# A deep-CTR tower on one core: row ids spread over the partitions by TensorE, start-up loads reordered by need, and fewer gathers between the first embeddings and the main loop

## The reference, cut to what matters

```python
e = jnp.stack([tbl_0[ids[:, 0]], ..., tbl_31[ids[:, 31]]], axis=1)   # 512 x 32 x 32
...
x0 = prev = e
for W in (filter_0, filter_1):                    # (1024, 128) and (4096, 128)
    z = jnp.einsum('bhd,bmd->bhmd', x0, prev)
    z = z.reshape(b, h * m, d)
    prev = jax.nn.relu(jnp.einsum('bpd,pn->bnd', z, W[0]))
    outs.append(prev)
z = jnp.sum(jnp.concatenate(outs, axis=1), axis=-1)        # 512 x 256
h = jnp.concatenate([z, dense_ctx], axis=1)
h = jnp.maximum(h @ W_top1 + b_top1, 0.0)
h = jnp.maximum(h @ W_top2 + b_top2, 0.0)
y = h @ W_top3
```

## Time and profile before

| | us |
|---|---|
| median of 3 runs (lowest, highest) | 889.67 (888.46, 891.25) |
| the profiled execution | 889.24 |
| its span, first to last instruction | 887.1 |
| PE busy in the span | 841.0 (95%) |
| DVE, ACT, POOL busy | 779.7, 764.0, 650.2 |
| PE's share of the chain that ended last | 89% |

### The profile page before, as it was taken

How to read it: one execution, slowest core, us unless ns; L and a number is a source line. 1 busy time by engine, 2 the same in 40 slices (tenths; PEclk the granted TensorE clock), 3 DMA queues, 4 the chain that set the end, 5 groups by cost and what they waited for, 6 DMA issues and landing times.

```text
span 887.1 us, 14536 instructions
## 1 busy us (share of the span) xinstructions
PE 841.0 (95%) x3637; PEld 678.5 (76%) x3637; DVE 779.7 (88%) x2420; ACT 764.0 (86%) x2582; POOL 650.2 (73%) x615
## 2 busy tenths in 40 slices
PE   0578999999999999999999999999999999999998
PEld 0346888888887888888888888888888888888873
DVE  2475999999999999999999999998899999999884
ACT  1239999999999999999999999999999999999872
POOL 6456888787788888888887888876766666676582
PEclk9979999999999999999999999999999999999999
DMA  7437767667767767667767666677767666675430
GB/s 181 106 75 199 176 155 163 147 153 170 161 153 168 163 152 163 147 157 166 162 153 174 161 154 161 144 164 160 160 154 170 155 155 156 143 165 106 92 72 0
DMA packets 53236, 131.20 MB, mean 148 GB/s; under 512 B 8395, under 2 KB 17875, under 8 KB 53028
## 3 DMA queue, kind: packets, MB, share of 16 engines
q0 software_dynamic: 21872, 68.43, 43.0%
q1 hardware_dynamic: 29502, 59.08, 20.3%
q10 hardware_dynamic: 1779, 2.77, 1.1%
HBM read 60.63 MB, written 3.05 MB: 72 GB/s over the span
## 4 chain that ended last, share of the span: by engine, by line
PE 89%; SPq 3%; DVE 3%; ACT 2%; DMA 2%; issue 1%; DVEq 0%
PE ya L870 14%; PE ya L872 14%; PE ya L871 14%; PE yd L870 11%; PE yd L872 11%; PE yd L871 11%; PE acc L870 3%; PE acc L872 3%; PE acc L871 3%; SPq L315 3%; ACT scaled L541 2%; DMA xb<-xt_scratch 1%; DVE emb L658 1%; DMA idx<-in_ids 1%; PE acc L899 1%
## 5 line engine op out<-in xcount | busy, mean ns | idle before, releaser
L541 ACT ACTIVATE scaled<-ya,emb 128x128 f32<-128x128 f32 x2288 | 654.3, 382 | 53.8 <-PE ya L872 46.0
L763 DVE SCALAR_TENSOR_TENSOR acc<-yd,emb,acc 128x128 f32<-128x128 f32 x1400 | 394.4, 341 | 5.9 <-PE yd L872 5.8
L406 POOL TENSOR_TENSOR quarter<-scaled 128x512 f32<-128x512 f32 x127 | 195.2, 1537 | 64.4 <-DMA scaled<-scaled 46.9
L870 PE MATMUL ya<-w_hi,prev_hi 128*128 128x512 f32 x572 | 224.8, 393 | 4.5 <-ACT scaled L541 2.5
L872 PE MATMUL ya<-w_hi,prev_lo 128*128 128x512 f32 x572 | 222.8, 390 | 0.0
L871 PE MATMUL ya<-w_lo,prev_hi 128*128 128x512 f32 x572 | 222.8, 390 | 0.0
L399 POOL DMA_DIRECT2D scaled<-scaled x127 | 116.4, 917 | 96.4 <-ACT scaled L541 91.7
L870 PE MATMUL yd<-w_hi,prev_hi 128*128 128x512 f32 x446 | 174.3, 391 | 1.0 <-DVE pooled_b L788 1.0
L872 PE MATMUL yd<-w_hi,prev_lo 128*128 128x512 f32 x446 | 173.6, 389 | 0.0
L871 PE MATMUL yd<-w_lo,prev_hi 128*128 128x512 f32 x446 | 173.5, 389 | 0.0
L381 POOL DMA_INDIRECT emb<-in_tbl,idx x112 | 123.2, 1100 | 42.7 <-issue 22.2
(11 more groups left out here) (136 smaller groups left out, 778.0 us busy)
## 6 DMA issues: line engine op xcount, KB each, us to landing
scaled<-scaled POOLq DMA_DIRECT2D x127, 512.0 KB, 8.3
xb<-xt_scratch SPq DMA_DIRECT2D x62, 512.0 KB
x<-xt_scratch SPq DMA_DIRECT2D x62, 192.0 KB
xm<-xt_scratch SPq DMA_DIRECT2D x30, 256.0 KB
scaled<-in_w ACTq DMA_DIRECT2D x4, 512.0 KB
emb<-in_tbl,idx POOLq DMA_INDIRECT x112, 3.9
xt_scratch<-xt_stage SPq DMA_DIRECT2D x7, 256.0 KB
wt_sb<-in_W_top SPq DMA_DIRECT2D x2, 512.0 KB
```

Source lines behind the costliest of these rows:

```text
L406: pool.tensor_tensor(four, piece[:, 0:C], piece[:, C:2 * C], ALU.add).then_inc(quartered, 1)
L541: op = act.activation(scaled[:, tile % PR, C * j + N * i:C * j + N * (i + 1)], a_bank(n)[:, N * i:N * (i + 1)], ACT.Copy, scale=scale_of(t ...
L763: dve.scalar_tensor_tensor(after, y_part, scale_of(tile, HB * j + i), before, ALU.mult, ALU.add).then_inc(chained, 1)
L870: pe.matmul(dst, v_hi, m_hi, start=start, stop=False)
```

## The change

Seven edits go together. `ids_across` is gone. In its place 8 KB of ids go to one partition (`ids_row`), VectorE turns them to float32 (`cast`), and TensorE multiplies them with a row of ones, which puts the ids of each half of a group on all partitions of a PSUM bank; `find` reads them there in four halves. The loads of w1 on ACT's queue wait until the small tables have landed. The ids of the later groups move from SP's queue, where they stood behind the tables, to ACT's, ahead of w1; and `number_within(1)` moves behind the first group's picks. The context's turn on TensorE moves behind the first group's candidates. `wt1_ctx` and the two biases with W_top3 (one array of 8 numbers per partition, made on the host) stay ahead of the loop; the two large tower weights move behind the loads of chunk 2 on SP's queue, and are waited for at the end. `fold_scale` rides on `pick`. GpSimd's gathers for group 1 wait for `l0_done` and are 5 where they were 13; the other 83 are spread over 80 tiles (1.04 a tile, before 0.94).

```diff
-    EARLY_NEXT = 13
+    EARLY_NEXT = 5
...
+        ids_row = sb("ids_row", [1, PICK_TILES, len(SMALL) * P], I32)
+        ones = sb("ones", [1, P])
+        ids_f32 = [xt_stage[0:1].rearrange("p g b -> p (g b)"), emb_sorted[0:1].rearrange("p g b -> p (g b)")]
+        across = [yd[:, 0, :], yd[:, 1, :], yd[:, 2, :], acc0[:]]
-        not_below = xt_stage[:].rearrange("p g b -> p (g b)")
+        not_below = sum0[:, 0, :]
...
         def _(sp):
             sp.dma_start(idx[:, 0, :], ids[0:P, :]).then_inc(ids_loaded, 16)
+            sp.dma_start(ids_row[:], ids_first...).then_inc(pick_loaded, 16)
             sp.dma_start(pick_sb[:], pick).then_inc(pick_loaded, 16)
-            sp.dma_start(ids_across[0:PICK_P], dram(ids_first, 0, [[0, PICK_P], [1, PICK_TILES * len(SMALL) * P]])).then_inc(
-                pick_loaded, 16)
...
-            sp.dma_start(idx[:, 1:BT, :], ids[P:B, :]...).then_inc(later_ids_loaded, 16)
-            sp.dma_start(wt1_sb[:], ...).then_inc(tower_loaded, 16)
...
+            sp.dma_start(wt1_ctx[:], W_top1[2 * N:2 * N + D_CTX, :]).then_inc(ctx_loaded, 16)
+            sp.dma_start(tower_small[:], biases_w3).then_inc(ctx_loaded, 16)
...
             load_l0(2)
+            sp.dma_start(wt1_sb[:], W_top1[0:2 * P, :].rearrange("(t p) n -> p t n", p=P)).then_inc(tower_loaded, 16)
+            sp.dma_start(wt2_sb[:], W_top2.rearrange("(t p) n -> p t n", p=P)).then_inc(tower_loaded, 16)
...
             pool.wait_ge(picked, PICK_TILES * len(PAIRS))
-            pool.wait_ge(gathered[0], 16 * GATHERED_LAST)
+            pool.wait_ge(l0_done, 1)
...
+            act.dma_start(idx[:, 1:BT, :], ids[P:B, :].rearrange("(t p) f -> p t f", p=P)).then_inc(later_ids_loaded, 16)
+            act.wait_ge(small_tables_loaded, 16 * len(SMALL))
             for s in range(4):
                 act.dma_start(w1_raw[:, fields, :], w1[:, fields, :]).then_inc(w1_loaded, 16)
...
-            act.wait_ge(tower_loaded, 16 * 6)
+            act.wait_ge(ctx_loaded, 32)
...
+            for bt in range(PICK_TILES):
+                pe.wait_ge(ids_cast, bt + 2)
+                for r in range(2):
+                    pe.matmul(across[2 * bt + r], ones[:], ids_f32[bt][:, C * r:C * (r + 1)], start=True, stop=True)
+                    ...
+            pe.wait_ge(small_tables_loaded, 16 * len(SMALL))
+            candidates(0)
+            ...   # the context's turn
+            candidates(1)
```

## The result

The changed kernel takes 887.76 us (median of 16 executions, 884.61 to 890.17), the kernel before 889.66 (888.18 to 891.25). The ratio is 0.9979, with a 95% interval of 0.9971 to 0.9988: 0.2% faster, which lies within the 0.3% that a measurement of this kernel can tell. Forecast were 875.5 us, with 872 to 881 as the range. The prediction was wrong by 12.3 us, and outside its range.

What follows compares the result with a forecast made beforehand. The first turn waited for picks, these for loads; TensorE bounds the loop behind. Moving the turn from 51.07 to 36.7 gains 14.4 us: span 872.7, plus 2.1 around it, 0.4 to the median, 0.3 for lateness: 875.5 us, range 872 to 881.

Steps and rivals of the forecast that it cites:

- Part 1: Ahead of the first turn: small tables, issued at 2.1 us, land 14.5 us later, at 16.5, likely 14 to 19.
- T: The time when the small tables land: forecast 16.5 us, likely 14 to 19; just under 33.17 before.
- Part 2: Work behind the small tables' landing: VectorE's picks end at 35.3 us, ScalarE's context share at 34.9.
- ScalarE: context's turn behind the candidates, T + 0.3 + 6.6 + 1.0: Context's turn, after landing to start 0.3 us and candidate matmuls 6.6; then copy and w0's rounding, 0.6 each.
- the picks' T + 18.8: VectorE's picks end 18.8 us after the small tables land, at 35.3: 17.8, 0.3 to start, 0.65 for a mask.
- Part 3: The first 24 gathers become last, landed at 36.1; first turn at 36.7 instead of 51.07, gain 14.4 us.
- The rule that the picks cost the gathers nothing: VectorE's reductions never hold the port shared with GpSimd, so gathers beside picks lose 0 us; bound at most 8.2.
- Part 4: First turn to loop stays 12.84 us, bounds -1 and +1; ScalarE's stage ahead of the full loop unchanged.
- The tower weights "0 to +1": 1 MB between loads of chunks 2 and 3, 4 to 5 us of DMA, chunk 3 wanted 20 us later: 0 to +1.
- Part 5: Gathers of later groups, spread over the loop's tiles, land in time for ScalarE's sort: cost 0, bound +1 us.
- The rivals: Tables still end it (0.20); picks or casts hold gathers (0.09); w1 ends it (0.06); picks never held the turn (0.01).
- what would show it wrong: Signs: turn waiting for `emb L670` or w1's rounding, gathers over 1.3 us before 34, or ScalarE idle before tile 20's sort.

Runs made afterwards that it cites:

- control: The changed kernel as it is, timed again on chip C beside the kernel before: 878.03 us, ratio 0.9878.
- again: The changed kernel as it is, timed once more on chip A: 878.09 us, beside 889.01 for the kernel before.

## Why the prediction was wrong, point by point

- *Part 1, T = 16.5.* Measured 16.07 in the result's trace, 14.4 to 16.1 in all traces with this order of loads. Right.
- *Part 2, what hangs on T.* This is where it failed, at "ScalarE: context's turn behind the candidates, T + 0.3 + 6.6 + 1.0" and at the picks' T + 18.8, both of which let a reader start when TensorE's matmul ends: the step put nothing for the wait between the two. Where completions come on time the terms hold: in `control` (T = 15.56) the copy starts at T + 5.7, w1's rounding at T + 8.3, and the picks end at T + 18.5. On the result's chip the copy starts at T + 19.4, w1's rounding at T + 20.4 though w1 had landed, and the picks end at T + 29.6. The last candidates are seen from 37.62 on; the second group's mask and four picks of 1.9 us each lead to 45.71 and the turn to 45.81. This costs 9.1 us against 36.7.
- *Part 3, the gathers end it, turn at 36.7.* Right where nothing is held: 35.43 and 35.84 in the two traces of the changed kernel, about 1 us early. The rule that the picks cost the gathers nothing held on every chip: 0.94 to 0.95 us each beside picks, the 24th at 32.77, earlier than the earlier trace rows. The one of 1.34 us (25.20 in `control`) lay beside L688 (25.04), which reads SBUF twice.
- *Part 4, turn to loop 12.84.* Measured 12.70. *The tower weights "0 to +1".* Mis-sized: I had asked when chunk 3 was wanted, and not how soon the x rows of chunk 2, just ahead of them on the queue, and of chunk 3, behind them, were. It cost up to 3.4 us, 1.8 and 2.5 in the two traces without the delay (45.9 and 46.6 against 44.0). The Trainium skill (DMA: Bandwidth & Descriptors, "Why a DMA increments its semaphore by 16 and not by 1"), which I had drawn on for 125 partitions, gives by the same rule three engines for these rows, whose slowest dimension is 3. No row here counts the engines: 12.5 and 17.5 us for a load of 192 KB don't speak against it, and don't show it.
- *Part 5, cost 0, bound +1.* The gathers came in time for the sort, as forecast. What I had not costed is GpSimd's own time. Before, 75 gathers over 80 tiles left tiles 0, 16, 32, 48 and 64 without one; 83 leave none free and put two into tiles 26, 53 and 79. Between banks 138 and 160 (tiles 31 to 35) this costs 2.0 us in the result's trace and 0.9 in `control`; VectorE's longer wait for GpSimd's sum (2.03 and 1.14 us, before 0.65) and its longer `small<-x` are the parts that the traces show.
- *The rivals.* None of the four is what happened. The first turn waited for `emb L670`, which the prediction had named as what would show it wrong, but not because T or the picks were slow.

Summed up: against 872.7 the span is 9.1 longer up to the turn, 0.2 shorter up to bank 0, 3.4 and 2.0 longer in the loop, 0.1 elsewhere: 887.1, measured 887.2. Where nothing is held the kernel takes 878.0, inside the range. There (`control`, span 875.5) the turn and the way to bank 0 are 1.8 us quicker than forecast, the two losses take 2.5 and 0.9, and 1.1 more goes between banks 160 and 566, which I did not trace. That the errors have different signs is luck, and so in part is the place inside the range.

What stays open: what holds the completions. Shown is that it went with the chip (887 us on chip B, 878 on A and C; chip D shows none either in the kernels run there), that it holds TensorE's completions and neither GpSimd's pace nor ScalarE's completions, and that at both places it ends when a long row of gathers ends. Chip B had a single comparison, so a chip and a state of that machine are not told apart. The profile's ends of matmuls are modelled, so it is not shown either whether the update is late or the matmul's own end; only the starts of the matmuls behind it are on time. That the gathers are the cause was only argued. The two experiments that would tell, gathers away and w1's loads away, were tried on chips where there was nothing to see, and not on chip B.

Against the gathers alone speaks that they run just as long on the other chips. The trace of the kernel before says more. By its record of semaphore events (below) it is of the same kind as the five with the delay, and its 13 gathers, from 51.73 to 71.71, run beside the first turns, layer 0 and the loop's first banks. Of the completions of TensorE that an idle engine waited for in that stretch only one is late, by 0.8 us. Its candidates start at 33.17, when its first row of gathers is nearly through (33.75), so there was little that could be held. This fits its 889 us on every chip. What the change did, then, was to move the candidates into a stretch where their completions can be late; the forecast took them over as rows of a stretch without that.

## What to carry to other kernels

A time that hangs on another engine's completion should be given a margin where the change moves it beside a long row of indirect DMAs (a precaution: the cause is not shown), and a change should be timed on more than one chip: here a gain of 11 us on two chips was 2.7 us on another. When a load is moved, ask for each later transfer on its queue how large its window is, the smallest first; a single buffer refilled once a chunk was the first to go late here. On an engine that has little time to spare, ask what tiles without extra work a denser spread takes from it.

## What the runs showed of the hardware

- TensorE's semaphore updates can be seen late by up to 13.3 us (turns over at 22.2, read at 35.50), on chip B and in the result's trace (whose chip is not in its record), and not on chips A, C and D. Four of them then arrive within 0.2 us (37.62 to 37.80), where their matmuls end 0.9 us apart.
- In the traces with the delay the record holds fewer semaphore events: 10,415 to 10,510 against 11,259 to 11,280 in the traces of the same program and its variants without it. Of the 782 events that the result's trace has less than `control` (10,496 against 11,278), 663 are landings of DMAs, and between 16 and 36 us, beside the gathers, it has 47 events where `control` has 374. A missing event is not the delay itself: the second pair of candidates left none in the result's trace (over at 19.84), and its pick started on time (20.10). Which is cause and which effect these runs don't tell. The trace of the kernel before has 10,579, and one late completion as well: its turn at L879 is over at 58.67, and ScalarE's copy starts at 59.48.
- The granted clock is 0.50 for 3.4 to 6.8 us at the loop's start or within 30 us behind it in some traces (48.18 to 51.6 in `again`, 63.13 to 69.96 with the turn behind the candidates, not in `control`). At half the pace that is an estimated 1.7 to 3.4 us of TensorE's time.
